# Transformer layer with routed experts on one core: full expert tiles run beside the last sequences' stages, 71 tiles instead of 72

## What is computed

```python
Q, K, V = heads(x @ Wq.T + bq), heads(x @ Wk.T + bk), heads(x @ Wv.T + bv)    # 16 heads of 8
probs = softmax(Q @ K.T / sqrt(8))
no0 = probs with the column of key 0 set to 0, divided by its row sum
attn = (probs + 0.5 * (no0 - probs)) @ V
x = layernorm(x + attn @ Wo.T + bo)
logits = x @ gate_w.T                                 # 8 experts
weights, selected = phi_routing(logits)               # the top 2 experts of each token
for e in range(8):
    h = silu(x @ w1[e].T) * (x @ w3[e].T)             # 128 -> 512
    out = out + wte[:, e:e + 1] * (h @ w2[e].T)       # 512 -> 128
x = layernorm(x + out)
```

## Time and profile before

| | us |
|---|---|
| time, median of 3 runs | 1476.93 (1476.47, 1476.93, 1479.99) |
| the profiled execution's own time | 1478.24 |
| its span in the profile | 1476.5 |
| TensorE busy | 1306.0 (88% of the span) |
| VectorE busy | 1031.3 (70%) |
| ScalarE busy | 815.5 (55%) |
| GpSimd busy | 717.5 (49%) |

### The profile page before, as it was taken

How to read it: one execution, slowest core, us unless ns; L and a number is a source line. 1 busy time by engine, 2 the same in 40 slices (tenths; PEclk the granted TensorE clock), 3 DMA queues, 4 the chain that set the end, 5 groups by cost and what they waited for, 6 DMA issues and landing times.

```text
span 1476.5 us, 22191 instructions
## 1 busy us (share of the span) xinstructions
PE 1306.0 (88%) x7184; PEld 673.0 (46%) x7184; DVE 1031.3 (70%) x1821; ACT 815.5 (55%) x1539; POOL 717.5 (49%) x771
## 2 busy tenths in 40 slices
PE   2899999999999999999999999953999999999930
PEld 1233332333333333333333333223999999999930
DVE  6668898989999889889998999743333333333348
ACT  1267765766766667667666677722444444444413
POOL 4223335354464354443644633453555555555567
PEclk9589998989998989889989999976999999999975
DMA  3322222222222223222223221323333333333338
GB/s 104 113 63 67 88 85 72 89 77 85 78 95 76 88 65 96 69 89 72 90 72 99 73 82 39 137 86 103 48 51 47 48 48 52 49 49 47 42 105 238
DMA packets 130881, 117.33 MB, mean 79 GB/s; under 512 B 17744, under 2 KB 116816, under 8 KB 130384
## 3 DMA queue, kind: packets, MB, share of 16 engines
q1 hardware_dynamic: 105664, 97.75, 22.2%
q0 software_dynamic: 25104, 18.15, 8.2%
HBM read 70.95 MB, written 45.42 MB: 79 GB/s over the span
## 4 chain that ended last, share of the span: by engine, by line
PE 65%; DVE 27%; issue 3%; DMA 2%; POOL 2%; SPq 1%; ACT 0%; DVEq 0%; ACTq 0%; POOLq 0%
DVE rowmax_sb L707 16%; PE acc_ps L453 11%; PE mx_ps L430 11%; PE ring_ps L441 10%; PE ring_ps L557 9%; PE mx_ps L534 9%; PE mx_ps L543 8%; PE ring_ps L473 1%; DVE TN_sb L716 1%; DVE absl_sb L795 1%; PE ring_ps L524 1%; PE ring_ps L470 1%; PE ring_ps L468 1%; PE ring_ps L487 1%; PE ring_ps L478 1%
## 5 line engine op out<-in xcount | busy, mean ns | idle before, releaser
L707 DVE TENSOR_REDUCE rowmax_sb<-mx_ps 128x2 f32<-128x1024 f32 x512 | 604.6, 1213 | 102.6 <-PE mx_ps L430 85.0
L586 ACT ACTIVATE probs_sb<-ring_ps 128x512 f32<-128x512 f32 x1024 | 563.0, 598 | 168.0 <-PE ring_ps L441 144.5
L441 PE MATMUL ring_ps<-region_sb 74*128 74x512 bf16 x1024 | 377.7, 401 | 2.4 <-ACT probs_sb L586 1.4
L430 PE MATMUL mx_ps<-region_sb 72*128 72x512 bf16 x1024 | 330.7, 407 | 30.8 <-DVE rowmax_sb L707 28.9
L453 PE MATMUL acc_ps<-probs_sb,values_sb 128*32 128x512 f32 x2048 | 291.2, 644 | 8.3 <-DVE TN_sb L716 8.2
L441 PEld LDWEIGHTS ring_ps<-region_sb 74*128 74x128 bf16 x1024 | 105.0, 103 | 247.9 <-ACT probs_sb L586 139.7
L648 ACT ACTIVATE region_sb<-region_sb 128x512 f32 x144 | 82.8, 622 | 226.3 <-PE mx_ps L543 212.2
L998 POOL CAST negmax_parts_sb<-negmax_sb 16x128 bf16<-16x128 f32 x64 | 18.0, 281 | 373.2 <-ACT negmax_sb L592 373.2
L430 PEld LDWEIGHTS mx_ps<-region_sb 72*128 72x128 bf16 x1024 | 99.9, 102 | 151.9 <-DVE rowmax_sb L707 59.7
L920 DVE TENSOR_SCALAR probs_sb<-ring_ps,probs_sb 128x128 f32<-128x128 f32 x144 | 43.9, 346 | 174.9 <-PE ring_ps L557 174.9
L1123 POOL DMA_INDIRECT x_d<-probs_sb x72 | 112.3, 1559 | 101.0 <-DVE probs_sb L920 79.7
(11 more groups left out here) (142 smaller groups left out, 1098.0 us busy)
## 6 DMA issues: line engine op xcount, KB each, us to landing
region_sb<-parts_d SPq DMA_DIRECT2D x384, 96.0 KB
probs_sb<-rows_d SPq DMA_DIRECT2D x72, 132.0 KB
parts_d<-q_parts_sb SPq DMA_DIRECT2D x16, 384.0 KB
parts_d<-k_parts_sb SPq DMA_DIRECT2D x16, 384.0 KB, 2.9
xT_sb<-xT SPq DMA_DIRECT2D x16, 256.0 KB, 3.1
x_sb<-x SPq DMA_DIRECT2D x16, 256.0 KB
x_d<-xn_sb SPq DMA_DIRECT2D x16, 256.0 KB, 3.3
y_d<-padrow_sb SPq DMA_DIRECT2D x16, 256.0 KB
```

Source lines behind the costliest of these rows:

```text
L430: last = nc.tensor.matmul(mx_ps[n % 2][:, i, :], QS[b % 2][0:KR, h, P * c:P * (c + 1)], KS[b % 2][0:KR, h, :], start=True, stop=True)
L441: nc.tensor.matmul(bank, KS[b % 2][0:KR + MR, h, P * c:P * (c + 1)], QS[b % 2][0:KR + MR, h, :], start=True, stop=True).then_inc(s_ring_re ...
L586: nc.scalar.activation(PT[u % 2][:, i // QC, i % QC, :], ring_bank("st", u, i), ACT.Exp, scale=SCALE).then_inc(s_ring_done, 1)
L707: V.tensor_reduce(rowmax[u % 2][:, 2 * k:2 * k + 2], mx_ps[n % 2][:, :, :], axis=AXX, op=ALU.max, negate=True).then_inc(s_mx_done, 1)
```

## The change

`PERIODS` ends with the last unit. What had to run in the periods behind it is spread over the first 14 tiles, in `tail(t)` of VectorE and GpSimd and `beside(t, place)` of TensorE:

- A first table is made in period 62, step 2, on VectorE, when 13 sequences are routed. It holds only full tiles, those whose 256 rows all come from these 13 sequences (counts rounded down). 13 sequences have 52 tiles' worth of rows, and 8 remainders of less than a tile add up to at most 7 tiles, so there are always at least 45 (`FIRST`). A second table at tiles 12 and 13 has the other 26 tiles (rounded up). The same count gives 71 tiles in all.
- The first tile's load waits for the scatters of 13 sequences and for the first table. The load of tile 45 waits for all scatters, the padding and the second table. The padding is stored ahead of the load of tile 22, W2 is loaded ahead of that of tile 6, and the last sequence's x1 is stored ahead of that of tile 11.
- The buffers that the tiles used in the probabilities of the last unit, and the tiles' W1 and W3, move to places that are free by then (a values buffer, the split parts, xT and full).
- The values of the last unit are multiplied in tile 0, "wo", "xt", "gl" and the two "px" in tiles 1 to 8, all through one PSUM bank. Scatter of sequence 13 is ahead of the output of tile 0 on GpSimd, that of 14 in tiles 6 and 7, that of 15 in tiles 12 and 13. The two last Exp of routing are ScalarE's in tiles 1 and 8, among its Silu.

The diff, cut to its core (`store_x1`, `zero_y`, `pad_ends`, `scatter`, `route` and the others keep their bodies):

```diff
-TILES = 2 * NT // TK + E
+TILES = 2 * NT // TK + E - 1
+ROUTED = NB - 3
+FIRST = 2 * ROUTED * L // TK - (E - 1)
...
-        XG = [carve(0, n * HALVES * ROW, HALVES * ROW).rearrange("p (w r) -> p w r", w=HALVES) for n in range(RING)]
-        at = RING * HALVES * ROW
-        XGT = [carve(0, at + n * TK, TK) for n in range(2)]
-        at += 2 * TK
+        values_flat = VE[0][:, :, :, :].rearrange("p c h v -> p (c h v)")
+        XG = [values_flat[:, n * HALVES * ROW:(n + 1) * HALVES * ROW].rearrange("p (w r) -> p w r", w=HALVES)
+              for n in range(RING)]
+        parts_flat = [t[:, :, :].rearrange("p t q -> p (t q)").bitcast(f32) for t in qk_parts]
+        XGT = [parts_flat[1][:, n * TK:(n + 1) * TK] for n in range(2)]
...
-        W1T, W3T = ([regions[3][:, (2 * n + k) * F:(2 * n + k + 1) * F] for n in range(2)] for k in range(2))
+        W1T, W3T = ([t[:, :] for t in ts] for ts in (xT_sb, full))
...
-        PERIODS = range(-3 * NG, (NB + 3) * NG)
+        PERIODS = range(-3 * NG, NB * NG)
...
+        TAIL_RING = {(1, 1): ("px", NB - 2), (3, 0): ("wo", NB - 1), (5, 1): ("xt", NB - 1),
+                     (6, 0): ("gl", NB - 1), (8, 1): ("px", NB - 1)}
+        TAIL = ring_count
+        for what in TAIL_RING.values():
+            ring_at[what] = ring_count
+            ring_count += 1
+        def bank_of(n):
+            return ring_ps[n % 3 if n < TAIL else 2][:, 0, :]
...
+            load_x(NB - 1)
+            sp.wait_ge(s_scattered, SPARE + SENT * ROUTED)
             sp.wait_ge(s_tab_done, 1)
-            sp.wait_ge(s_pv_ready, UNITS)
+            sp.wait_ge(s_pv_ready, UNITS - NG)
...
+                if t == RING:
+                    sp.wait_ge(s_ring_ready, ring_at["st", UNITS - 1, 15] + 1)
+                    sp.dma_start(W2[:, :], w2T).then_inc(s_w2, 16)
+                elif t == RING + 5:
+                    store_x1(NB - 1)
+                    zero_y(NB - 1)
+                elif t == RING + 16:
+                    pad_ends()
+                elif t == FIRST:
+                    sp.wait_ge(s_scattered, SPARE + SENT * NB)
+                    sp.wait_ge(s_pad, 16 * E)
+                    sp.wait_ge(s_tab_done, 2)
...
+            def beside(t, place):
+                if t == 0:
+                    for c in (0, 1) if place == 0 else (2, 3):
+                        values(UNITS - 1, c)
+                if (t, place) in TAIL_RING:
+                    behind(*TAIL_RING[t, place])
+            pe.wait_ge(s_tab_done, 1)
+            pe.wait_ge(s_ring_done, TAIL)
+            pe.wait_ge(s_mx_done, STEPS * UNITS)
...
+                beside(t, 0)
                 if is_tile(t + 1):
                     tile_in(t + 1)
                 if is_tile(t - 1):
                     tile_down(t - 1)
                 if is_tile(t):
                     tile_lin(t)
+                beside(t, 1)
...
+            act.wait_ge(s_split, 2 * NB)
             copy_weights(0)
+            act.wait_ge(s_parts_stored[1], 16 * NB)
...
+                if t == 0:
+                    act.wait_ge(s_pv_ready, UNITS - 1)
                 nc.scalar.activation(SG[t % 2], up_ps, ACT.Silu).then_inc(s_silu, 1)
                 if is_tile(t + 1):
                     tile_in(t + 1)
+                if t in (1, 8):
+                    routing_exp(NB - 2 if t == 1 else NB - 1)
+                for place in range(2):
+                    if (t, place) in TAIL_RING:
+                        behind(*TAIL_RING[t, place])
...
+            def tile_table(first, last):
+                ge, gn = tile_by_expert(first, last)
...
+                tb(V.tensor_tensor(ge, tile_no[:, 0:last - first].unsqueeze(2).to_broadcast([1, last - first, E]),
+                                   by_tile(cum), ALU.is_ge))
+                tb(V.tensor_reduce(expert[:, which], ge, axis=AXX, op=ALU.add))
+                tb(V.tensor_tensor(gn, ge, by_tile(move), ALU.mult))
+                tb(V.tensor_reduce(no, gn, axis=AXX, op=ALU.add))
+                tb(V.tensor_tensor(no, tile_no[:, 0:last - first], no, ALU.add))
...
+            def first_tables():
+                dve.wait_ge(s_parts_stored[0], 16 * NB)
+                tb(V.tensor_tensor(cnt, offs[0:1, 0, :], eoff[0:1, :], ALU.subtract))
+                whole_tiles(cnt)
+                running_sum()
+                tb(V.tensor_scalar(move, tiles, -1.0, None, ALU.mult))
+                tile_table(0, FIRST)
+                tb(V.tensor_scalar(upto, cum, float(FIRST), None, ALU.min))
+                tb(V.tensor_copy(taken[:, 0:1], upto[:, 0:1]))
+                tb(V.tensor_tensor(taken[:, 1:E], upto[:, 1:E], upto[:, 0:E - 1], ALU.subtract))
...
+                    if (p, k) == (UNITS - 2, 2):
+                        first_tables()
+            def tail(t):
+                if t == 0:
+                    sums_by_query(UNITS - 2)
+                    route(NB - 2, 0)
+                    route(NB - 2, 1)
+                elif t == 1:
+                    sums_by_query(UNITS - 1)
+                    reciprocals(NB - 1)
+                    route(NB - 2, 2)
+                    route(NB - 2, 3)
+                elif t == 2:
+                    route(NB - 2, 4)
+                    attn_to_rows(NB - 1)
+                elif t == 3:
+                    route(NB - 2, 5)
+                elif t == 4:
+                    route(NB - 2, 6)
+                    ln_stats(NB - 1)
+                    ln_moments(NB - 1)
+                elif t == 5:
+                    ln_apply(NB - 1)
+                elif t in (7, 8):
+                    route(NB - 1, 2 * (t - 7))
+                    route(NB - 1, 2 * (t - 7) + 1)
+                elif t in (9, 10, 11):
+                    route(NB - 1, t - 5)
+                elif t == 12:
+                    V.tensor_copy(end_i[:, :], offs[0:1, 0, :]).then_inc(s_ends, 1)
+                    rest_by_expert()
+                elif t == 13:
+                    rest_by_tile()
...
+            def tail(t):
+                b = NB - 1
+                if t == 0:
+                    pool.wait_ge(*rows_in(0))
+                    for s in range(2):
+                        scatter(b - 2, s)
+                    add_bo(b)
+                elif t == 1:
+                    normalise(b)
+                elif t == 3:
+                    residual(b)
+                elif t == 4:
+                    inverse_deviation(b)
+                elif t == 5:
+                    send_x(b)
+                elif t in (6, 7):
+                    scatter(b - 1, t - 6)
+                elif t in (12, 13):
+                    scatter(b, t - 12)
             for t in range(TILES):
+                tail(t)
                 pool.wait_ge(s_y, t + 1)
                 if t < 2:
-                    pool.wait_ge(*((s_x1_stored, 16 * NB), (s_zeroed, 16 * NB))[t])
+                    pool.wait_ge((s_x1_stored, s_zeroed)[t], 16 * (NB - 1))
                 else:
+                    if t in (FIRST, FIRST + 1):
+                        pool.wait_ge((s_x1_stored, s_zeroed)[t % 2], 16 * NB)
```

More of the change, by code:

```diff
@@ L623, in behind, with routing_exp @@
                 done.then_inc(s_ring_done, 1)
+            def routing_exp(b):
+                act.wait_ge(s_rt, RT * b + 14)
+                nc.scalar.activation(expd[:, :, :, :], dist[:, :, :, :], ACT.Exp, scale=-1.0).then_inc(s_expd, 1)
             for p in PERIODS:
@@ L850, in route, with tb, whole_tiles @@
                     V.tensor_copy(pos[:, :, :], posf[:, :, :]).then_inc(s_rt, 1)
+            step_of_tab = [0]
+            def tb(ins):
+                step_of_tab[0] += 1
+                ins.then_inc(s_tab, 1)
+                dve.wait_ge(s_tab, step_of_tab[0])
+            cnt, tiles, cum, taken, move, upto = (tabc[:, n, :] for n in range(6))
+            tile_no, expert, row0, woff = (tab[:, n, :] for n in range(4))
+            def whole_tiles(n):
+                tb(V.tensor_copy(tabi[:, :], n))
+                tb(V.tensor_scalar(tabi[:, :], tabi[:, :], TK.bit_length() - 1, None, ALU.logical_shift_right))
+                tb(V.tensor_copy(tiles, tabi[:, :]))
```

107 lines of the change are left out of this document (54 added, 53 removed).

## The result

| | before | after |
|---|---|---|
| median of the runs (us) | 1478.46 (4 runs, beside after) | 1428.04 (4 runs, 1420.11 to 1435.05) |
| ratio, 95% interval | | 0.9687 [0.9638, 0.9735]: faster |
| profiled execution: own time / span (us) | 1478.24 / 1476.5 | 1435.05 / 1433.3 |
| last exponential ends | 968.3 | 970.7 |
| first `up` | 1021.0 | 972.4 |

The account below looks back on a forecast made before the run. It took TensorE alone to bound the tiles, with time to be had in the 52.7 us gap before them. Terms summed to -45.1 us, from the median 1476.93 to 1431.8 us, range 1425 to 1445.

Parts of the forecast that it names:

- (1): Between attention's last exponential and the first `up`: the first `up` moves from 1021.03 to 970.3, -50.7 us.
- (2): Chain of tiles: one tile less, -5.5 us.
- (3): Tile 0 on TensorE: values of unit 63 add 4.3 us; first `up` left unchanged, or -1.6 if the clock holds.
- (4): Early tiles on TensorE: five stage products ("wo", "gl", "xt", two "px") stand in its path, +3.7 us.
- (6): Tiles 2 to 5: VectorE's `y` and `h` wait for GpSimd, stalls of 0.4, 1.1 and 1.6 us, +3.1 in sum.
- (7): GpSimd's scatters and SP's pad stores: 6.6 us of scatter lateness hidden by 10 us of row-load cover, pads hidden too, 0.
- (8): W2's load before the first `down`: issued at about 969, landing at 977.5, 4 us of cover, 0.
- (9): VectorE in period 62: the first table takes 6.7 us, but TensorE wants the delayed normalised x later still, 0.
- (10): Final stage behind the tiles: waits for the last accumulations as before, 0.
- C: Rival for the 71 tiles: without the rest before them they run at attention's clock or less, making the change slower; chance 0.03.
- D: Rival for the first tile: held by a count that comes only with sequence 13 or later, 1438 to 1455 us; chance 0.03.
- B: Rival for the early tiles: the relay feeds on itself or load cover is too thin, 1439 to 1450 us; chance 0.20.

Follow-up runs that it names:

- e2_71_only: The kernel before with 71 tiles in place of 72 and nothing else changed: 1474.91 us, ratio 1.0003 to the kernel before.
- e10_w2_early: The changed kernel with relay two tiles a step, scatters two a tile, a quarter of the last values earlier, W2 behind three row loads: 1435.83 us.
- e5_route_late: The changed kernel with sequence 14's routing moved from tiles 0 to 4 to 6 to 10, later scatters and pad stores, relay kept: 1434.6 us.
- e1_again: The changed kernel once more, unaltered: 1435.3 us, ratio 0.9763 to the kernel before.
- both controls: The changed kernel run again, unaltered, in the second and third sets: 1430.13 and 1430.16 us.
- e4_ring5: The changed kernel with five buffers for the tiles' rows instead of six: 1442.18 us, ratio 0.982 to the kernel before.
- e7_best: The changed kernel with relay two tiles a step, scatters two a tile and a quarter of the last values ahead of the first `up`: 1428.38 us.
- e6_w2_behind: The changed kernel with another 2 MB load ahead of W2 on its queue, the first `down` waiting for both: 1438.51 us.

## Why the prediction was right, and where it was not

**(1) The gap, -50.7.** Right: 52.7 became 1.7, so -51.0, with ScalarE's copy of the rows last, as named. e2_71_only, where 50.5 us of gap stayed, shows that it comes from the order.

**(2) One tile, -5.5.** -4.5 in e2_71_only, -5.5 without its longer half clock (its first `up` took 3.78 us, not 3.31); the steps of 5.46 us stand by the forecast.

**(3) The last values, +4.3, and the first `up`.** Two pairs of chunks take 1.92 us each in the timeline and add 1.85 each in the chain, +3.7. The first `up` was left at 3.31, with -1.6 as the other end; the clock held, and it took 1.99: -1.3. This was the term that I chose wrongly: the wait of 1.11 us ahead of it did not bring the half clock.

**(4) The products, +3.7.** The four long steps of e10_w2_early, where nothing else stands, are 5.9 + 6.4 + 6.7 + 5.9 = 24.9, less four of 5.46: +3.1.

**(5) VectorE's other work, 0.** Right: by e5_route_late it is not what stalls.

**(6) The relay, +3.1.** The three stalls are where they were named. In after the steps give 0.7 + 0.1, 1.0 and 1.8 (7.01 - 5.46 - 0.9; 5.56 - 5.46; 6.47 - 5.46; 8.53 - 5.46 - 1.3), 3.6 in sum against 0.4 + 1.1 + 1.6, and spreading the relay takes them away.

**(7) The scatters and the pads, 0.** Right: no load came late. The scatters left 2.5 us of cover at tile 19, 3.4 by the forecast. The pad stores were called hidden without a sum: with some 10 us on SP and GpSimd 3 us late, the 10 us of cover would not have held them. They took 8.8 us and have 0.2 to 0.7 us to spare, which e5_route_late used up. That they were hidden was luck.

**(8) W2, 0 with 4 us of cover.** The sum held by luck. The failing step is "W2 is issued at about 969": it named the six row loads ahead of it and didn't cost them. They take 6.56 us of SP's queue and start at 966.22, so the issue was at 972.83; and the 2 MB took 9.1 us, not 8.5. The cover was 0.3 us.

**(9) The first table, 0.** The table takes 7.0 us on VectorE (951.7 to 958.7; 6.7 forecast, though the count of its small steps was low, 17 for 22), and in the last 20 us of attention TensorE waits for ScalarE alone, 1.4 us, as before. Whether it costs anything in the whole time no run separates. **(10) The final stage, 0.** It was 1.3 us longer. The second sum of GpSimd in it starts 12.8 us after the last `down` (12.1 before), and the last store takes 2.9 us to land (2.3 before); why, no run separates.

In sum: -51.0 - 5.5 + 3.7 - 1.3 + 3.1 + 3.6 = -47.4 by the measured terms, and the stretch says -46.9; the forecast had -45.1, and from profile to profile the time fell by 43.2. Against the median the forecast is 3.8 us high; by the ratio on the median then shown it is 0.9687 x 1476.93 = 1430.7. The closeness of these last numbers is in part luck, since the changed kernel's medians lie from 1428.0 to 1435.3 over four sets; what the runs bear out is the terms.

**The rules weighed.** The routing beside `normalise` was held, as this row of after shows, from VectorE's timeline:

```profile
987.88 3.40 DVE L886 TENSOR_SCALAR dest_sb<-dest_sb 128x8 f32<-128x8 f32 x1
```

It is a step of one input that is 0.17 us elsewhere. The Trainium skill, SBUF — State Buffer, "Who interferes with whom", also lists `tensor_scalar` and `copy` among the operations that can take the shared port; I had weighed only its sentence on two inputs. Either way it cost nothing: it ended at 991.28 and VectorE then waited 1.34 us for GpSimd's attention rows. In e10_w2_early, `route` meets `normalise` too (3.40 us for the same step) and the step of the tile stays 5.5. ScalarE's change of table is 1.28 us in each of the four places around the two Exp (983.47, 988.04, 1027.87, 1032.44 in the timeline of after), with the tiles' steps beside both pairs 5.9 in e10_w2_early, which is 5.46 and the 0.45 of "px". The 0.6 us of stall for each pair, which were worked out from the Trainium skill, ScalarE: Activation LUTs, "What ACT_TABLE_LOAD costs", did not show: the Exp starts at 984.76, where the change of table ends at 984.75, so no drain stands between, nor ahead: the change starts 0.02 us behind the copy before it (983.45). (The 0.6 does not come out of its numbers either: by the Trainium skill's 2.66 us a switch, twice, less the two changes' own 2.56 and the 1.5 to spare, the estimate is 1.3 a pair.)

**The rivals.** C (the clock falls) is out: the half clock is granted for 0 us from the first `up` to the last `down` of after. D is out by the first `up` at 972.39. Of B, the relay did not feed on itself: it is over at tile 5. Its other half, cover too thin, was nearer than its 0.20 said: 0.3 us at W2 and 0.2 to 0.7 us at the pads. The 7 us of e1_again are no case of it: there TensorE waited for neither rows nor W2.

## What to carry to other kernels

Work that only one engine at a time can do belongs beside work that another engine is full with; here 50 us of relay cost 3.6 us of stalls, beside 6.8 of TensorE's own work, once it stood beside tiles, and with two tiles for each hand-over the stalls were gone. To say when a load is issued, add up what stands on its queue ahead of it (six issues of 1.1 us here) and not only the semaphore that it waits for. To say that something is hidden, sum its lateness against the cover each time; two of the terms called 0 here had less than 1 us to spare. And where the clock moves the whole time by 1%, compare a stretch of the profile that begins behind the disturbed part.

## What the runs showed of the hardware

- What a wait of TensorE in the tiles did to the granted clock: waits of 0.85 and 1.5 us left it full in after and both controls. A wait of 1.62 us in e4_ring5 was followed by 3.4 us at half, one of 2.05 us in the same profile by none; one of 2.03 us in e1_again and one of 2.13 in e7_best by 3.4 each. In that of 5.01 us in e6_w2_behind the half clock began within the wait and lasted 6.8 us. So the length of the wait alone does not tell.
- VectorE steps of 128x8 elements took 3.40 us (L886) and 2.48 us (L903) beside GpSimd's operations instead of 0.17, with one input; L886 was held through an indirect transfer's issue and two multiplications of `normalise`. In e7_best a step of two inputs took 3.05 us beside the same `normalise`:

```profile
983.43 3.05 DVE L875 TENSOR_TENSOR factor_sb<-kept_sb,expd_sb 128x64 f32<-128x64 f32 x1
```

- On one chip, in the tiles behind GpSimd's indirect writes, what waited for TensorE was released 2 to 3 us after the matmuls' ends in the trace, in three kernels; on the chips of the two other sets never. It cost e1_again some 5 us.
- W2's 2 MB took 9.1 us to land behind six loads of rows in after (8.7 to 9.6 in the other kernels of sets 2 and 3 that issue it alone there), 8.8 behind three, but 11.1 in e7_best.
- GpSimd's closing drain took 2.9 to 3.0 us in eight kernels and 6.5 to 7.0 us in the five whose edit touches GpSimd's program, and there it ended the span. Why is open.
